# Decoder stack: the projection first in a turn, another order on four engines, and V in high and low parts for two units at a time

## The reference, cut to what matters

```python
x = shift(x); qkv = x @ Wqkv; q, k, v = split(qkv, 3)      # 16 heads of 64
q, k = l2norm(q) * qs, l2norm(k) * ks
q = q * cos * scale + rotate_half(q) * sin * scale
k = k * cos / scale + rotate_half(k) * sin / scale
sim = 8 * (q @ k.T)             # windows of 32 queries against 64 keys, masked
out = softmax(sim) @ v
x = x + out @ Wo
h = layernorm(x) @ W1 + b1; a, gate = split(h, 2)           # 341 + 341 columns
x = x + (a * gelu(gate)) @ W2 + b2
```

## Time and profile before

| | |
|---|---|
| three runs | 1365.84, 1370.93, 1378.49 us |
| profiled execution, its own time | 1366.57 us |
| its span, and granted TensorE clock | 1363.8 us, 0.948 |
| PE busy | 1174.1 us (86%) |
| PE weight loads | 726.5 us (53%) |
| DVE busy | 942.8 us (69%) |
| ACT busy | 838.3 us (61%) |
| POOL busy | 658.7 us (48%) |
| DMA | 107.08 MB, mean 79 GB/s |

### The profile page before, as it was taken

One profiled execution on the slowest core, in us unless ns is written; L12 is line 12 of the kernel. 1 busy time (PEld: TensorE's weight loads), 2 busy tenths in 40 slices (PEclk: granted clock), 3 DMA queues, 4 the chain that ended last, 5 costly groups with the idle time before them and its releaser, 6 DMA issues. The chain is left out here.

```text
span 1363.8 us, 26023 instructions
## 1 busy us (share of the span) xinstructions
PE 1174.1 (86%) x9636; PEld 726.5 (53%) x9636; DVE 942.8 (69%) x1207; ACT 838.3 (61%) x1260; POOL 658.7 (48%) x522
## 2 busy tenths in 40 slices
PE   7787869998557988898889989999888989999975
PEld 3222347786224655566555655656555655656551
DVE  2788957775736776776777767767776776767733
ACT  4553456664345668675776667775776767676744
POOL 1555524442326555645555555645555555555420
PEclk9887989999868999999999999999999999999997
DMA  3000035100203532444233432444233432434220
...
DMA packets 75507, 107.08 MB, mean 79 GB/s; under 512 B 25347, under 2 KB 31938, under 8 KB 75002
## 3 DMA queue, kind: packets, MB, share of 16 engines
...
## 5 line engine op out<-in xcount | busy, mean ns | idle before, releaser
L1667 POOL TENSOR_TENSOR st_sq_sum<-h 128x512 f32<-128x512 f32 x96 | 127.3, 1327 | 235.1 <-ACT h L1420 235.1
L1604 DVE TENSOR_REDUCE st_mx<-banks 128x8 f32<-128x512 f32 x96 | 66.4, 692 | 201.4 <-PE banks L1305 201.1
L1671 POOL TENSOR_TENSOR mo_w<-mo_w,x 128x512 f32<-128x512 f32 x96 | 122.1, 1272 | 160.1 <-DVE mo_w L1540 160.1
L1420 ACT ACTIVATE h<-banks 128x1024 f32<-128x1024 f32 x96 | 98.4, 1025 | 157.8 <-PE banks L1270 157.5
L1278 PE MATMUL banks<-st_sq_sum,head_ones 128*128 128x512 f32 x192 | 108.4, 647 | 41.5 <-POOL st_sq_sum L1667 41.5
L1290 PEld LDWEIGHTS banks<-st_wv,stream 128*128 128x128 f32 x768 | 102.3, 194 | 48.4 <-issue 47.8
L1539 DVE TENSOR_TENSOR x<-banks,st_scaled 128x1024 f32<-128x1024 f32 x96 | 117.0, 1219 | 14.3 <-ACT h L1420 12.8
L1550 DVE SCALAR_TENSOR_TENSOR st_turned<-st_rn,mo_w 128x1024 f32<-128x1024 f32 x96 | 120.9, 1259 | 5.4 <-ACT st_rn L1431 2.8
L1672 POOL TENSOR_TENSOR mo_w<-mo_w,x 128x512 f32<-128x512 f32 x96 | 122.2, 1272 | 0.0
L1329 PEld LDWEIGHTS banks<-st_p_blocks,st_vs 128*64 128x64 f32 x1536 | 77.8, 137 | 74.0 <-issue 72.6
L1540 DVE TENSOR_TENSOR mo_w<-banks,st_scaled 128x1024 f32<-128x1024 f32 x96 | 116.5, 1213 | 0.0
...
## 6 DMA issues: line engine op xcount, KB each, us to landing
...
```

The costliest lines, as they stand in the source:

```text
L1667: nc.gpsimd.tensor_tensor(sq_sum[:], sq[:, 0, :], sq[:, 1, :], ALU.add).then_inc(sq_summed.sem, 1)
L1671: nc.gpsimd.tensor_tensor(cos_part[:, which, 0, :], cos_part[:, which, 0, :], sin_part[:, 1, :], ALU.subtract).then_inc(add_done.sem, 1)
```

## The change

V is projected two units at a time, and one turn earlier (unit t+2 in turn t). A turn of the pair does two token tiles of 128 for four heads (256 columns). Input and weights are split as for q and k: three fp32r passes each over 256 columns, with the high and low input as the stationary operand. That makes six passes a turn in place of eight. For this V's weights are split too, one of four parts behind every second part of q and k: four more CASTs on DVE and four more subtractions on POOL a layer. `vn` and `vs` hold two units in each half, the shifted copy is stored in odd turns only, with twice the bytes, and V's weights are loaded once a layer at t = 3 instead of in two halves at t = 11 and t = 15.

The order in a turn is another on all four engines:

- PE: (stage 3: the third value product) projection, (stage 0: output projection) scores, (stage 2: two value products) turning, output projection, (mean, first gate product or down projection) V, head norm, (stage 2: third gate product) values, (stage 0: variance; stage 1: second gate product).
- ACT: square, copies of the probabilities, copy of V, logarithm, exponential, root, (stage 0: square of the centred rows) copy of the output. Before, the exponential came second, and the centred square stood last.
- DVE: sum and reciprocal for unit t, (stage 3: gated product) norm, (residual, or scaling) rope products, (centring; stage 2: two gated products) maximum and difference for unit t+1, CASTs of the weights, second residual.
- POOL: product of the probabilities for unit t, sum of squares, additions of the rope products, low halves of the weights.

Three feed-forward tiles (`xn`, `act`, `gate`) move into memory that earlier parts leave free. The core of the diff:

```diff
-        self.w_raw, self.wv, self.wo = sb("w_raw", [P, 8, 2 * P]), sb("wv", [P, 8, P]), sb("wo", [P, 8, P])
+        self.w_raw, self.wv_raw, self.wo = sb("w_raw", [P, 8, 2 * P]), sb("wv_raw", [P, 4, 2 * P]), sb("wo", [P, 8, P])
...
-        self.qT, self.vs = sb("qT", [P, 2, 2, SEQ]), sb("vs", [P, 2, 4, P])
+        self.qT, self.vs = sb("qT", [P, 2, 2, SEQ]), sb("vs", [P, 2, 4, 2 * P])
...
-    def load_v(self, sp, d, layer, half):
-        pairs = slice(4 * half, 4 * half + 4)
-        sp.dma_start(self.wv[:, pairs, :], at_layer(d["w_v"], layer)[:, pairs, :]).then_inc(self.wv_in[half].sem, 16)
+    def load_v(self, sp, d, layer):
+        sp.dma_start(self.wv_raw[:], at_layer(d["w_v"], layer)).then_inc(self.wv_in.sem, 16)
...
+    SPLITS = PARTS + PARTS // 2
+
+    def qk_split(i):
+        return i + i // 2 + 1
+
+    def v_split(g):
+        return 3 * g + 3
...
         def shift_values(s, n):
-            r = n % 2
-            sp.wait_ge(*v_copied.at(s.turn, n + 1))
+            r = n // 2 % 2
+            sp.wait_ge(*v_copied.at(s.turn, n + 2))
             sp.dma_start(vs[32:128, r, :, :], vn[0:96, r, :, :]).then_inc(vs_in[r].sem, 16)
             sp.dma_start(vs[0:32, r, 1:4, :], vn[96:128, r, 0:3, :]).then_inc(vs_in[r].sem, 16)
...
-                if t >= -1 and s.unit(t + 1):
+                if t >= -1 and t % 2 == 1 and s.unit(t + 1):
...
+                        places.load_v(sp, d, turn + 1)
...
         def project_v(s, n, job, stage):
 
-            b, pair = n // 8 % 2, n % 8
+            b, g, half = n // 8 % 2, n % 8 // 2, n % 2
             if v_copied.any(s.turn, n):
                 pe.wait_ge(*v_copied.at(s.turn, n))
             if stage in (2, 3):
                 pe.wait_ge(*act_done.at(s.turn, 3 * job + stage))
-            pe.wait_ge(*wv_in[pair // 4].at(s.turn, 16 * (n // 16) + 16))
-            for tile in range(4):
-                rows = slice(P * tile, P * tile + P)
-                last = mm(V_BANK[:, rows], Y[:, b, rows], wv[:, pair, :], start=True, stop=True)
+            if n % 16 < 8 and half == 0:
+                pe.wait_ge(*w_split.at(s.turn, SPLITS * (n // 16) + v_split(g)))
+            if n % 8 == 0:
+                pe.wait_ge(*y_low_done.at(s.turn, n // 8 + 1))
+            for i in range(2):
+                rows = slice(P * (2 * half + i), P * (2 * half + i) + P)
+                out = V_BANK[:, 2 * P * i:2 * P * i + 2 * P]
+                mm(out, y_high[:, b, rows], wv_high[:, g, :], start=True, stop=False)
+                mm(out, y_high[:, b, rows], wv_low[:, g, :], start=False, stop=False)
+                last = mm(out, y_low[:, b, rows], wv_high[:, g, :], start=False, stop=True)
             last.then_inc(v_done.sem, 1)
...
         def body(s):
             for t in s.range:
                 job, stage = s.stage(t)
-                if stage == 1:
-                    variance(s, job)
+                if stage == 3:
+                    up_value(s, t, job, 2)
+                if s.unit(t + 4):
+                    project(s, t + 4)
+                if stage == 0 and s.unit(t - 1):
+                    out_proj(s, t - 1)
                 if t >= -1 and s.unit(t + 1):
                     scores(s, t + 1)
-                if s.unit(t + 4):
-                    project(s, t + 4)
                 if stage == 2:
                     up_value(s, t, job, 0)
                     up_value(s, t, job, 1)
-                if stage == 3:
-                    up_value(s, t, job, 2)
                 if s.unit(t) and t >= 0:
                     turn_probs(s, t)
-                if t >= 0 and s.unit(t - 1):
+                if t >= 0 and stage != 0 and s.unit(t - 1):
                     out_proj(s, t - 1)
-                if t >= -1 and s.unit(t + 1):
-                    project_v(s, t + 1, job, stage)
+                if stage == 0:
+                    mean(s, job)
+                if stage == 1:
+                    up_gate(s, t, job, 0)
+                if stage == 3:
+                    down(s, job)
+                if t >= -2 and s.unit(t + 2):
+                    project_v(s, t + 2, job, stage)
                 if s.unit(t + 4):
                     head_norm(s, t + 4)
-                if stage == 0:
-                    mean(s, job)
-                if stage in (1, 2):
-                    up_gate(s, t, job, 0 if stage == 1 else 2)
-                if stage == 3:
-                    down(s, job)
+                if stage == 2:
+                    up_gate(s, t, job, 2)
                 if s.unit(t) and t >= 0:
                     values(s, t)
+                if stage == 0:
+                    variance(s, job)
                 if stage == 1:
                     up_gate(s, t, job, 1)
...
         def copy_v(s, n):
-            r = n % 2
+            r, half = n // 2 % 2, n % 2
             ac.wait_ge(*v_done.at(s.turn, n + 1))
-            if pv_done.any(s.turn, n - 1):
-                ac.wait_ge(*pv_done.at(s.turn, n - 1))
-            if vs_in[r].any(s.turn, 32 * (n // 2)):
-                ac.wait_ge(*vs_in[r].at(s.turn, 32 * (n // 2)))
-            A(vn[:, r], V_BANK.rearrange("p (j f) -> p j f", f=P), ACT.Copy).then_inc(v_copied.sem, 1)
+            if half == 0:
+                if pv_done.any(s.turn, n - 2):
+                    ac.wait_ge(*pv_done.at(s.turn, n - 2))
+                if vs_in[r].any(s.turn, 32 * (n // 4)):
+                    ac.wait_ge(*vs_in[r].at(s.turn, 32 * (n // 4)))
+            A(vn[:, r, 2 * half:2 * half + 2, :], V_BANK.rearrange("p (j f) -> p j f", f=2 * P), ACT.Copy).then_inc(v_copied.sem, 1)
...
                     A(rstd[:], rstd[:], ACT.Exp, scale=-0.5).then_inc(rstd_step.sem, 1)
                 if s.unit(t + 4):
                     square(s, t + 4)
+                if s.unit(t) and t >= 0:
+                    copy_probs(s, t)
+                if t >= -2 and s.unit(t + 2):
+                    copy_v(s, t + 2)
+                if s.unit(t + 4):
+                    logarithm(s, t + 4)
                 if t >= -1 and s.unit(t + 1):
                     n = t + 1
                     ac.wait_ge(*sub_done.at(s.turn, n + 1))
                     A(prob[:, n % 2], prob[:, n % 2], ACT.Exp, scale=QK_SCALE).then_inc(exp_done.sem, 1)
-                if s.unit(t) and t >= 0:
-                    copy_probs(s, t)
-                if t >= -1 and s.unit(t + 1):
-                    copy_v(s, t + 1)
                 if s.unit(t + 4):
-                    logarithm(s, t + 4)
                     root(s, t + 4)
-                if t >= 0 and s.unit(t):
-                    copy_out(s, t)
                 if stage == 0:
                     ac.wait_ge(*centre_step.at(s.turn, 3 * job + 1))
                     if stat_done.any(s.turn, 2 * job):
                         ac.wait_ge(*stat_done.at(s.turn, 2 * job))
                     A(dsq[:], dx[:], ACT.Square).then_inc(rstd_step.sem, 1)
+                if t >= 0 and s.unit(t):
+                    copy_out(s, t)
...
             v.tensor_copy(w_high[:, i, :], w_raw[:, i, :]).then_inc(w_high_done.sem, 1)
+            if i % 2 == 1:
+                g = i // 2
+                dv.wait_ge(*places.wv_in.at(s.turn, 16 * ahead + 16))
+                if ahead:
+                    dv.wait_ge(*v_done.at(s.turn, 10 + 2 * g))
+                v.tensor_copy(wv_high[:, g, :], wv_raw[:, g, :]).then_inc(w_high_done.sem, 1)
...
+                if s.unit(t) and t >= 0:
+                    totals(s, t)
+                if stage == 3:
+                    gated(s, job, 2)
                 if t >= -3 and s.unit(t + 3):
                     normalise_heads(s, t + 3)
+                if stage == 0:
+                    residual1(s, job)
+                if stage == 1:
+                    scale_centred(s, job)
+                if s.unit(t + 4):
+                    rotate(s, t + 4)
+                if stage == 0:
+                    centre(s, job)
+                if stage == 2:
+                    gated(s, job, 0)
+                    gated(s, job, 1)
+                if t >= -1 and s.unit(t + 1):
+                    from_maximum(s, t + 1)
                 if s.first and t + 5 < PARTS:
                     high_weights(s, t + 5, 0)
                 if t >= PARTS - 1 and t < 2 * PARTS - 1 and not s.last:
                     high_weights(s, t - PARTS + 1, 1)
-                if stage == 0:
-                    residual1(s, job)
-                if stage == 1:
-                    scale_centred(s, job)
-                if stage == 2:
-                    gated(s, job, 0)
-                    gated(s, job, 1)
-                if stage == 3:
-                    gated(s, job, 2)
-                if s.unit(t + 4):
-                    rotate(s, t + 4)
-                if t >= -1 and s.unit(n):
-                    dv.wait_ge(*exp_done.at(s.turn, n + 1))
-                    if rec_done.any(s.turn, n - 1):
-                        dv.wait_ge(*rec_done.at(s.turn, n - 1))
```

(20 more changed lines are left out.)

135 lines of the change are left out of this document (69 added, 66 removed).

## The result

| | before | after |
|---|---|---|
| median of four runs | 1369.06 us | 1404.29 us (1402.63 to 1406.77) |
| ratio, 95% interval | | 1.0264 [1.0232, 1.0296] |
| profiled execution: time, span, granted clock | 1366.57, 1363.8, 0.948 | 1402.63, 1400.8, 0.921 |

The changed kernel is slower by 2.6%, outside the range of 1335 to 1396 us; 1372 us and no difference were forecast.

The account below looks back on a forecast made before the run. Plain turns were taken as bound by PE, feed-forward turns by a chain over the engines. Plain turns -44, feed-forward +32, start +6 and clock +12 made +6 on 1366.57: 1372 us, no measurable difference, range 1335 to 1396.

Parts of the forecast that it names:

- The plain turn of 6.8 us: Turns without a feed-forward part: 6.8 us (6.75 to 7.25) instead of 7.9; with the last layer's, together -44 us.
- the ring: Plain turns: the chain over the engines from DVE's products to ACT's output copy and next square has .2 us of slack.
- V's passes: V on PE: six fp32r passes over 256 columns replace eight and take .75 us a turn.
- The rival of slow weight loads: V on PE: weight loads show, 1.15 us instead of .75, +18 us, 1390 us in all; chance 10%.
- Casts: DVE's weight casts beside POOL's additions take up to 1.39 us: one adds .2 us a turn, two add 1.0.
- Third feed-forward turn: V waits for DVE's gated products behind the rope products; PE idle from 5.9 to 9.3, turn 13.05 us.
- Moved at nothing: V's shifted store in double-size pieces and V's single weight load at t = 3 cost nothing, both hidden.
- First, second, fourth turn: Feed-forward groups: turns of 11.0, 8.5 and 12.7 us, the fourth 14.9 where the rope table is scaled too.
- The clock: PE at 1.2 GHz behind idle stretches: about 1.4 us each, 11 times behind the third turn's wait; +12 us.
- The rival of the clock: Each idle stretch of 2 us or more brings 1.2 GHz, 33 falls at 1.4 us: 1394 us; chance 18%.
- the rival without loss: Feed-forward turns lose nothing and no new clock falls: 1333 us, or 1350 halfway; chance 30%, whole or in part.
- The start: First seven turns: POOL's low half of the weights comes after two additions, 62.5 us instead of 56.7; +6 us.

Follow-up runs that it names:

- a_port: Changed kernel with the head norm's logarithm and root kept in PSUM instead of an SBUF tile: 1383.52 us, 1.0113 of the kernel before.
- best_high: Changed kernel with norm from PSUM, gated products first, the start's weight splitting as before, stream's high part ahead of scaling and output copy: 1303.80 us, 0.9516 of before.
- a_v32: Changed kernel with V again a plain fp32 product and no splitting of V's weights, all orders kept: 1409.68 us, 1.0312 of the kernel before.
- a_start: Changed kernel with the first layer's weight halves split where the kernel before had them, in the first seven turns: 1399.94 us, 1.0237 of before.

## Why the prediction was wrong, step by step

- **The plain turn of 6.8 us failed.** The step was the ring and "POOL's probabilities (at 2.4 of the next turn, needed at 2.83)". That 2.4 took the product at the 1.04 us it has in the kernel before. In the new order DVE does totals and then norm, so the norm and POOL's product are released by the same reciprocal and run side by side, and the product takes 2.02 us. It ends at 3.3 of the turn (1121.82 against 1118.53) instead of 2.4, and the turn is 7.44. In the stretches of plain turns a_port gives 15 us of the missing 28 back, and over the whole pipeline 20.
- The other 13 us of these turns are what a_port still lacks. 13 lie at the heads of turns 4 and 12: 6.9 and 7.8 were forecast, 8.74 and 9.15 measured. The projection there waits for the high part at the end of the fourth turn, and the clock falls behind that wait. Turns 5 and 13 cost another 10, turn 13 as told below and turn 5 in the first layer, where in the changed kernel the scores wait 2.83 us for the transfer of k. Against these stand 10 us by which the kernel before, over all layers, is longer than the two stretches of the earlier trace rows that the sum multiplied. The stretch of turns 4 to 7 already held a turn 4 of 8.5 us; that it should become 6.9 was given no reason. In a_port turn 4 lasts 7.18 us in some layers and 8.75 in others, with the same work, and in best_high 7.18 to 7.20 in every layer but the first: such a fall costs 1.6. My sum had falls in the third turns alone.
- **V's passes:** .75 forecast, .71 measured. By the Trainium skill ("TensorE: Matmul & The Clock Gate", the part on 56 ns instead of 53.3 ns) it would be .66; the measured value lies between. The rival of slow weight loads is out: .19 of load stays hidden at a step of .12.
- **No idle time before the head norm:** right. Before it stood 41.5 us of idle in all, now 7.0.
- **Casts:** one or two a turn were to take 1.39 and to cost up to 1.0 in turns 12 and 14. V's casts do take it in 14 of 24 (mean 918 ns), those of q and k never: five of 48 take .9, the others .28 (mean 346). But they are not what makes turns 13 and 14 long (7.87 and 8.33): a_v32, which has no cast of V, has 7.86 and 8.50 there. The lines below are of turns 13 and 14 of the changed kernel, the last of a_v32's turn 14.

```profile
1194.00 2.18 ACT L1451 ACTIVATE st_scaled<-st_table,st_rope_scale 128x1024 f32<-128x1024 f32 x2
1196.08 1.01 ACT L1433 ACTIVATE h<-banks 128x1024 f32<-128x1024 f32 x1
...
1202.12 0.73 POOL L1683 TENSOR_TENSOR st_w_low<-st_w_raw,st_w_high 128x256 fp32r<-128x256 f32 x1
1204.89 0.66 PE L1325 MATMUL banks<-ident,mo_w 128*128 128x128 f32 x4 [1.32 <-POOL mo_w L1694]
```

```profile
1210.74 0.66 PE L1326 MATMUL banks<-ident,mo_w 128*128 128x128 f32 x4 [1.36 <-POOL mo_w L1685]
```

  ACT scales the rope table of turn 12 ahead of turn 13's square, which starts 3.3 us into the turn (which began at 1192.77) instead of 1.7. The exponential is late by it, and POOL's low half of the weights stands ahead of the product, so PE waits 1.3 us in turn 14, with V's casts or without. The sum had neither step.
- **Third feed-forward turn:** V held from 5.9 to 9.3, 3.4 us, by the gated products. 3.10 measured, same mechanism. The turn was put at 13.05 and a fall of 1.4, and lasts 15.3; where a_port has no fall in it, it lasts 13.66.
- **Moved at nothing** (V's shift and V's load): right but for one turn. The waits for V's shifted copy are 1.3 us in the whole run, as before, and PE's wait for transfers of k falls from 17.1 us to 2.8, all in turn 5 of the first layer; whether V's load caused that one isn't traced.
- **First, second, fourth turn:** 11.0, 8.5, 12.7 (14.9 with scaling) forecast; 10.67, 8.64, 11.7 (13.8) measured. In the group t 8 to 11 the second turn is 10.2, again a fall of the clock, behind the wait for the variance.
- **The clock.** This term was mis-sized. Some 11 new falls were counted for +12. Between first and last projection the clock's record has 31 stretches at half clock, as long as the last of the rows above, where the kernel before has 10. The 11 behind the wait for V, which the forecast counted, are there. The others stand in or behind the wait for the high part (before turn 12 in all five layers, before turn 4 in four of five), behind PE's wait of 2.3 us for ACT's square ahead of the variance (six of 11 first turns) and in the start. What I held against it was a misreading: group t 8 to 11 has 1.00 only because the earlier trace rows cut it before its fall. PE idles 2.00 us before turn 12, and behind that the clock fell in the kernel before too, in four of five layers:

```profile
1153.60:1157.00 3.40, 3.40 (x11) 2.16 (x10) 3.40 (x5) 2.61 (x4) 1.35 (x1) 0.50 0.08 19
```

  Length alone doesn't decide: pieces of 3.1 us were followed by a fall in 11 of 11 cases, pieces of 1.83 in four of five, pieces of 2.26 to 2.28 before the variance in five of six in one group and one of five in the other.
- **The rival of the clock was added up wrongly.** 33 falls are 46 us in place of the counted 12; the sum took 33 for them and left the 12 out. By its own terms it is 1366.6 - 44 + 32 + 6 + 46 = 1407, and the range would have reached beyond 1404. That would have been luck: it keeps the -44 that came as -16, and counts 33 falls where some 21 were added. In the same way the rival without loss is 1366.6 - 44 + 6 = 1329 and not 1333.
- **The start:** 62.5 us forecast, 65.0 measured: POOL's low half behind its additions, as said. a_start shows the cause by undoing it.
- **Feed-forward turns lose nothing** (30%): out. It was one move away: with the gated products first, these turns and the last layer's three take 468.2 us, where the kernel before takes 466.7.

In sum: of the 31 us between forecast and the profiled execution, the plain turns make 28, the feed-forward turns 8 and the start 2; front and end take 8 off. The loss in the feed-forward turns was foreseen with its place, and its size (52 for 44) is the sum of two misses: without falls the groups would be 44.7 and 46.8 us (an estimate from turns without one), 7 less in all than forecast, and the falls then make 27 where 12 were counted. The gain that was to pay for it did not come, because a duration was carried over from an order in which the instruction had other neighbours. I had named the shared ports for the cast and looked for no other pair. The norm and the product are the costliest such pair: 80 us of POOL, where V's long casts make 15 of DVE.
